# A three-layer feature-interaction network in fp32: half chunks moved to the front of a layer, products made two chunks wide

## The chip, the cores and the metric

The kernel runs on one core of a Trainium2 chip. The metric is the device time of one execution in microseconds (us); the time of a kernel is the median of its runs.

## The reference, cut to what matters

The input is 2048 samples of 39 fields with 16 channels, fp32. Each layer multiplies all pairs of a previous and an original field, channel by channel, and mixes the products with a learned matrix to 128 features. The first 64 features are kept, the other 64 feed the next layer.

```
z = relu(einsum('bhk,bmk,hmf->bfk', prev, x0, Wr) + b_i)   # i = 0, 1, 2
results.append(z[:, :64]); prev = z[:, 64:]                # prev = x0 for i = 0
y = sum_k(concatenate(results, axis=1)) @ W_lin
```

## The kernel before, in words

**Tiling.** The batch is cut into 32 blocks of 64 samples; a block is 1024 columns (16 channels x 64 samples). The contraction over pairs (h, m) is cut into chunks of up to 128 rows, one pair a row. For each chunk VectorE multiplies two 1024-column operands elementwise into a product, and TensorE multiplies the chunk's weights with it, 512 columns at a time. An fp32 matmul is two instructions in the profile.

**Layer 0** works on symmetric pairs of the input: 6 full chunks (x_rot, C0) and one half chunk (x_rot_s) that has 64 rows for each half of the columns. `split` does the two halves of such a chunk with two matmuls on rows 0 to 63 and 64 to 127 of the array, which can run side by side. `full` does two matmuls on all rows.

**Layers 1 and 2** have 20 chunks each (CH): 10 with the first spread of the previous layer's features (a = 0, t = 0 to 8, then T2), 9 with the second spread (a = 1), and last the chunk T1, which has 64 rows of work. In layer 1 it is a split chunk whose product VectorE makes with two instructions (L216); in layer 2 it is 64 rows high (L212). The other 19 are 128x1024 products (L210). Layer 2 keeps only 64 features, so its two column halves go to the two 64-column halves of the array and run side by side (L362). The products go through a ring of 10 slots (prod); VectorE waits for a free slot with chunk_used, TensorE for a product with prod_ready. layer2 waits at chunk 18 for the products of chunks 18 and 19 together (L359).

**Order, by engine.** It is written out by hand; each engine has its own program, and semaphores tie them. TensorE, per block i: layer 1 of i (76 full instructions at L323, 4 split at L317), layer 0 of block i+1 (split chunk first, then 24 full instructions), layer 2 of i (80 instructions). VectorE: products1(i), channel_sum2(i), products0(i+1) with the split product at L195 first, products2(i) with the channel sum of layers 0 and 1 (L258) after its chunk 11. ScalarE takes the results out of PSUM: evacuate1 writes the spread of layer 1 (prev; two ops at L404, four at L409) and the kept half (res01, L416), evacuate0 the same for layer 0, evacuate2 layer 2's (L434); weigh01 and weigh2 scale the sums into a pool. Layer 2's products can't start before evacuate1's first two ops. SP issues all input loads: load_pairs (operands of layer 0) when layer 0 has been done, load_bc (x_bc, fields repeated over partitions, double-buffered by block parity u) when VectorE has made layer 2's products.

**Start.** Block 0 has no x_bc loads: VectorE builds it from x_seed by shuffles (seed, L189), most of them between the products of layer 0. keep_warm issues matmuls on zeros.

**End.** The last layer 1 is put into the middle of layer 2 of the block before, after its chunk 10 (TAIL = 11 chunks before it, 9 behind it), so that TensorE has work while ScalarE spreads the result. At the very end two small matmul groups (L393), a copy and one store make the output.

Of the kernel before, what the change touches and what calls it, by code (L numbers as in the profile page):

```python
# [14 lines left out]
def cin_kernel(nc, x, w0, w0_mirror, w1, w2, b0, b1, b2, w_lin, out, dims):  # L15
# [14 lines left out]
    CH = len(CHUNKS)  # L30
    X0_GROUPS = [(0, 1), (1, 2), (2, 4), (4, C0)]
# [8 lines left out]
    BC_LOADS = [QPT] * len(XB_GROUPS) + [3]  # L40
    SMALL = 7
    TAIL = RING + 1
# [3 lines left out]
    with ExitStack() as ctx:  # L46
# [28 lines left out]
        res01 = sb("res01", [P, NB])  # L75
# [17 lines left out]
        w2_loaded = sem("w2_loaded")  # L93
        small_loaded = sem("small_loaded")
        ones_ready = sem("ones_ready")
        split_loaded = sem("split_loaded")
        rep_loaded = sem("rep_loaded")
# [4 lines left out]
        bc_loaded = [[sem(f"bc_loaded{u}{g}") for g in range(len(XB_GROUPS) + 1)]  # L102
# [3 lines left out]
        chunk_used = sem("chunk_used")  # L106
        acc0_full = sem("acc0_full")
# [14 lines left out]
        def _(sp):  # L122
# [5 lines left out]
            def load_pairs(i):  # L128

                for h in range(NH):  # L130
# [4 lines left out]
                    sp.dma_start(x_rot_s[rows, :], src).then_inc(split_loaded, 16)  # L135
                for r, n in ((0, 48), (48, 48), (96, ROWS0[0] - 96)):
                    sp.dma_start(x_rep[r:r + n, :], x[i, r % M:r % M + n, :]).then_inc(rep_loaded, 16)
# [8 lines left out]
            def load_bc(i, u):  # L146
# [5 lines left out]
                for q in range(2):  # L152
                    src = rows_of(i, QPT * T + q, [[0, HALF], [1, NB]])
                    sp.dma_start(x_bc[HALF * q:HALF * q + HALF, u, T2, :], src).then_inc(bc_loaded[u][-1], 16)
                src = rows_of(i, M - 1, [[0, P], [1, NB]])
                sp.dma_start(x_bc[:, u, T1, :], src).then_inc(bc_loaded[u][-1], 16)
# [5 lines left out]
            sp.wait_ge(acc0_full, 1)  # L162
            load_pairs(1)
            load_bc(1, 1)
            for i in range(U):
                sp.wait_ge(acc0_full, i + 2)
                load_pairs(i + 2)
                sp.wait_ge(prod_ready, i * (2 * CH) + 2 * CH)
                load_bc(i + 2, i)
            with sp.Fori(1, STEPS - 1) as j:  # L170
                for u in range(U):
                    i = j * U + u
                    sp.wait_ge(acc0_full, i + 2)
                    load_pairs(i + 2)
                    sp.wait_ge(prod_ready, i * (2 * CH) + 2 * CH)
                    load_bc(i + 2, u)
# [7 lines left out]
        def _(dve):  # L184
# [7 lines left out]
            def products0(i, seeds=()):  # L192

                dve.wait_ge(split_loaded, i * (32 * NH) + 32 * NH)
                nc.vector.tensor_tensor(x_rot_s[:], x_rot_s[:], x_rep_s[:], ALU.mult).then_inc(prod0_ready, 1)  # L195
                dve.wait_ge(rep_loaded, i * (16 * 3) + 16 * 3)
                for g, (c0, c1) in enumerate(X0_GROUPS):
                    dve.wait_ge(rot_loaded[g], i * (16 * ROT_LOADS[g]) + 16 * ROT_LOADS[g])
                    for c in range(c0, c1):
                        r = x_rot[0:ROWS0[c], c, :]  # L200
                        nc.vector.tensor_tensor(r, r, x_rep[0:ROWS0[c], :], ALU.mult).then_inc(prod0_ready, 1)  # L201
                        for t in seeds[c:c + 1]:
                            seed(t)

            def product(layer, c, u, slot):

                a, t = CHUNKS[c]
                old, new = prev[layer - 1][a], x_bc[:, u, t, :]
                if t < T1:
                    mul = nc.vector.tensor_tensor(prod[:, slot, :], old[:], new, ALU.mult)  # L210
                elif layer == 2:
                    mul = nc.vector.tensor_tensor(prod[0:HALF, slot, :], old[0:HALF, :], new[0:HALF], ALU.mult)  # L212
                else:
                    for h in range(NH):
                        k, n = slice(HALF * h, HALF * h + HALF), slice(BANK * h, BANK * h + BANK)
                        mul = nc.vector.tensor_tensor(prod[k, slot, n], old[k, n], new[k, n], ALU.mult)  # L216
                mul.then_inc(prod_ready, 1)

            def products1_seeded():

                spread_by = {T2: T + 2, T1: T + 3}
                for c, (a, t) in enumerate(CHUNKS):
                    if a == 0 or t == T1:
                        dve.wait_ge(seed_spread, spread_by.get(t, t + 1))
# [318 lines left out]
```

## Time and profile before

| | |
|---|---|
| Median of 3 runs | 2055.02 us (2054.32 to 2055.65) |
| Profiled execution, its own time | 2055.68 us |
| Its span | 2053.9 us |
| TensorE / weight loads | 2030.3 / 804.6 us busy (99% / 39%) |
| VectorE / ScalarE / GpSimd | 1809.6 / 539.0 / 1.2 us busy (88% / 26% / 0%) |
| Input loads | 307.71 MB, 68.7% of the DMA engines' time |
| Granted TensorE clock | 0.997 of full speed over the span |

The span is measured from the first to the last instruction in the trace; the device time holds 1.8 us more. In the profile PE is TensorE's matmuls, PEld its weight loads (they overlap the matmuls), DVE VectorE, ACT ScalarE, POOL GpSimd, SP the engine that issues loads. L323 is line 323. A matmul's listed duration (some 593 ns) holds its way through the array and is longer than the distance to the next one. "[0.76 <-issue]" behind a row is the idle time before it on its engine and what ended it.

### The profile page before, as it was taken

What the parts mean: (1) busy time and instruction counts of PE and PEld (TensorE: products, weight loads), DVE (VectorE), ACT (ScalarE), POOL (GpSimd) and SP (SyncE); (2) the same over time, 40 slices, a digit from 0 to 9 for tenths busy, and PEclk for the clock granted to TensorE, in tenths of its full rate; (3) what the DMA queues carried; (4) which work ended last, traced back from release to release, by engine and by line L of the source; (5) the groups of instructions that cost most, each with busy time, mean ns of one, the idle gap of its engine ahead of it and who ended that gap; (6) DMA issues with size and microseconds to landing.
All of it is one profiled execution on the core that took longest, in us unless ns stands there. A gap on an engine that the chain in (4) does not pass through costs nothing.

```text
span 2053.9 us, 20773 instructions
## 1 busy us (share of the span) xinstructions
PE 2030.3 (99%) x6050; PEld 804.6 (39%) x6050; DVE 1809.6 (88%) x1630; ACT 539.0 (26%) x547; POOL 1.2 (0%) x5
## 2 busy tenths in 40 slices
PE   7999999999999999999999999999999999999998
PEld 2344333443333443334433344333344333443342
DVE  6988988889988889888899888898888988889987
ACT  1331133311333212333113332123321233311322
POOL 0000000000000000000000000000000000000000
PEclk9999999999999999999999999999999999999999
DMA  8967866668766688666786666876668866668710
GB/s 199 199 146 163 179 145 140 148 146 190 158 130 150 144 176 169 150 139 144 157 190 142 140 147 143 187 166 133 147 145 168 183 141 141 145 148 190 152 38 0
DMA packets 98550, 308.99 MB, mean 150 GB/s; under 512 B 19252, under 2 KB 19252, under 8 KB 98408
## 3 DMA queue, kind: packets, MB, share of 16 engines
q1 hardware_dynamic: 97400, 307.71, 68.7%
q10 hardware_dynamic: 1136, 1.12, 0.2%
q8 instruction: 6, 0.10, 0.0%
q14 instruction: 8, 0.07, 0.0%
HBM read 308.74 MB, written 0.01 MB: 150 GB/s over the span
## 4 chain that ended last, share of the span: by engine, by line
PE 89%; DVE 6%; issue 3%; ACT 0%; DVEq 0%
PE acc L323 66%; PE acc L362 20%; DVE prod L210 4%; PE acc L317 3%; DVE prod L212 2%; ACT prev L404 0%; DVE sum L258 0%; DVE x_bc L189 0%; DVEq L241 0%; PE acc_y L393 0%; DVE x_rot L201 0%; ACT res L434 0%; DVE x_seed L305 0%; ACT pool L439 0%; DVEq L240 0%
## 5 line engine op out<-in xcount | busy, mean ns | idle before, releaser
L210 DVE TENSOR_TENSOR prod<-prev,x_bc 128x1024 f32<-128x1024 f32 x1216 | 1390.1, 1223 | 221.6 <-ACT prev L404 215.0
L323 PE MATMUL acc<-prod,w_sb 128*128 128x512 f32 x2432 | 1052.3, 593 | 0.3 <-DVE prod L210 0.3
L323 PEld LDWEIGHTS acc<-prod,w_sb 128*128 128x128 f32 x2432 | 459.4, 190 | 592.6 <-issue 546.8
L362 PE MATMUL acc<-prod,w_sb 128*64 128x512 f32 (+1 forms) x2560 | 569.3, 596 | 6.1 <-DVE prod L212 1.2
L323 PE MATMUL acc<-x_rot,w_sb 117*128 117x512 f32 (+1 forms) x768 | 341.0, 599 | 2.7 <-DVE x_rot L201 2.7
L362 PEld LDWEIGHTS acc<-prod,w_sb 128*64 128x64 f32 (+1 forms) x2560 | 175.3, 136 | 396.2 <-issue 320.1
L409 ACT ACTIVATE prev<-acc,bias 32x1024 f32<-32x1024 f32 x256 | 283.4, 1107 | 4.0
L404 ACT ACTIVATE prev<-acc,bias 64x1024 f32<-64x1024 f32 x128 | 142.0, 1109 | 498.6 <-PE acc L317 355.2
L201 DVE TENSOR_TENSOR x_rot<-x_rot,x_rep 117x1024 f32<-117x1024 f32 (+1 forms) x192 | 221.1, 1220 | 3.0 <-DMA x_rot<-x 2.9
L323 PEld LDWEIGHTS acc<-x_rot,w_sb 117*128 117x128 f32 (+1 forms) x768 | 143.4, 190 | 198.8 <-issue 189.7
L439 ACT ACTIVATE pool<-sum,wl_col 128x64 f32 (+1 forms) x65 | 22.1, 342 | 679.6 <-DVE sum L258 679.6
L258 DVE TENSOR_REDUCE sum<-res 128x64 f32<-128x512 f32 (+1 forms) x65 | 96.5, 1484 | 2.9 <-ACT res L434 2.0
L434 ACT ACTIVATE res<-acc,bias 128x512 f32<-128x512 f32 x32 | 22.1, 690 | 292.4 <-PE acc L362 292.4
L416 ACT ACTIVATE res<-acc,bias 64x1024 f32<-64x1024 f32 x64 | 70.9, 1108 | 26.6 <-DVE sum L258 25.0
L216 DVE TENSOR_TENSOR prod<-prev,x_bc 64x512 f32<-64x512 f32 x64 | 44.1, 689 | 0.9 <-PE acc L323 0.5
L317 PE MATMUL acc<-x_rot_s,w_sb 64*128 64x512 f32 x128 | 33.8, 606 | 8.7 <-DVE x_rot_s L195 8.7
L212 DVE TENSOR_TENSOR prod<-prev,x_bc 64x1024 f32<-64x1024 f32 x32 | 38.9, 1217 | 0.5 <-PE acc L323 0.5
L317 PE MATMUL acc<-prod,w_sb 64*128 64x512 f32 x128 | 36.1, 641 | 0.0
L317 PEld LDWEIGHTS acc<-x_rot_s,w_sb 64*128 64x128 f32 x128 | 12.5, 191 | 24.1 <-issue 24.1
L195 DVE TENSOR_TENSOR x_rot_s<-x_rot_s,x_rep_s 128x512 f32<-128x512 f32 x32 | 21.8, 682 | 0.0
L317 PEld LDWEIGHTS acc<-prod,w_sb 64*128 64x128 f32 x128 | 9.6, 184 | 24.3 <-issue 23.5
L189 DVE STREAM_SHUFFLE x_bc<-x_seed 128x1024 f32<-128x1024 f32 (+1 forms) x12 | 15.5, 1296 | 0.0
(17 smaller groups left out, 21.8 us busy)
## 6 DMA issues: line engine op xcount, KB each, us to landing
x_bc<-x SPq DMA_DIRECT2D x310, 256.0 KB, 13.1
x_bc<-x SPq DMA_DIRECT2D x155, 512.0 KB, 21.2
x_rot<-x SPq DMA_DIRECT2D x192, 312.0 KB
x_rot<-x SPq DMA_DIRECT2D x192, 156.0 KB
x_bc<-x SPq DMA_DIRECT2D x124, 128.0 KB, 8.9
x_rep<-x SPq DMA_DIRECT2D x64, 192.0 KB
x_rep_s<-x SPq DMA_DIRECT2D x64, 128.0 KB, 2.6
x_rot_s<-x SPq DMA_DIRECT2D x64, 128.0 KB, 2.8
```

The costliest lines, as they stand in the source:

```text
L201: nc.vector.tensor_tensor(r, r, x_rep[0:ROWS0[c], :], ALU.mult).then_inc(prod0_ready, 1)
L210: mul = nc.vector.tensor_tensor(prod[:, slot, :], old[:], new, ALU.mult)
L212: mul = nc.vector.tensor_tensor(prod[0:HALF, slot, :], old[0:HALF, :], new[0:HALF], ALU.mult)
L216: mul = nc.vector.tensor_tensor(prod[k, slot, n], old[k, n], new[k, n], ALU.mult)
L258: return nc.vector.tensor_reduce(total[:], res[:].rearrange("p (k b) -> p b k", b=BB), mybir.AxisListType.X, ALU.add)
L317: mm = nc.tensor.matmul(acc[:, h, :], w[k, :], rhs[h], start=start, stop=stop)
L323: mm = nc.tensor.matmul(acc[:, h, :], w, rhs[:, BANK * h:BANK * h + BANK], start=start, stop=stop)
L362: mm = nc.tensor.matmul(acc2[HALF * h:HALF * h + HALF, :], w2_sb[0:k, c, :], prod[0:k, c % RING, BANK * h:BANK * h + BANK], start=(c == 0) ...
L404: op = nc.scalar.activation(dst[0][HALF * g:HALF * g + HALF, :], src, ACT.Relu, bias=bias[HALF:P, layer:layer + 1])
L409: op = nc.scalar.activation(dst[1][QUAD * q:QUAD * q + QUAD, :], acc[h:h + QUAD, :, :].rearrange("p h n -> p (h n)"), ACT.Relu, bias=bias[ ...
L416: nc.scalar.activation(res01[HALF * layer:HALF * layer + HALF, :], acc[0:HALF, :, :].rearrange("p h n -> p (h n)"), ACT.Relu, bias=bias[0: ...
L434: nc.scalar.activation(res2[:], acc2[:], ACT.Relu, bias=bias[:, 2:3]).then_inc(res2_ready, 1)
```

## The change

- The chunks of layers 1 and 2 are taken in the order ORDER: chunk T1 first, then the others as before. RUNS groups them by position: 4 single chunks and 8 pairs. A pair is one VectorE product of 2 x 1024 columns whose first operand is repeated by a broadcast; prod_ready counts runs (12 a layer), chunk_used still counts chunks.
- TensorE does layer 1's split chunk first, and right behind it the split chunk of layer 0 of the next block (layer0_split); its other layer-0 chunks keep their place after layer 1. In block 0 and in the last layer 1 the two stay apart (ahead=False).
- VectorE makes the split product of layer 0 before products1. SP loads its operands on their own (load_split) when TensorE has used the old ones.
- The weights of layer 2's chunk T1 are set to zero in rows 64 to 127 (GpSimd, once), and its product and its matmul take all 128 rows.
- res01 has two buffers (the second is x_seed), and the channel sum of layers 0 and 1 of block i-1 is done in block i, between products0(i+1) and products2(i). weigh01 moves with it.
- TAIL is 12 chunks (8 runs) and the seeds of block 0 are dealt out anew.

The core of the diff (removed lines are mostly left out, they stand above):

```diff
     T2, T1 = T, T + 1
     CHUNKS = [(0, t) for t in range(T)] + [(0, T2)] + [(1, t) for t in range(T)] + [(0, T1)]
     CH = len(CHUNKS)
+    ORDER = [CH - 1] + list(range(CH - 1))
+    RUNS = [(0, 1), (1, 1), (2, 2), (4, 2), (6, 2), (8, 2), (10, 1), (11, 1), (12, 2), (14, 2), (16, 2), (18, 2)]
+    RUN_OF = [n for n, (_, w) in enumerate(RUNS) for _ in range(w)]
+    NR = len(RUNS)
...
-    BC_LOADS = [QPT] * len(XB_GROUPS) + [3]
+    BC_T1, BC_T2 = len(XB_GROUPS), len(XB_GROUPS) + 1
+    BC_LOADS = [QPT] * len(XB_GROUPS) + [1, 2]
     SMALL = 7
-    TAIL = RING + 1
+    TAIL_RUNS, TAIL = 8, 12
     LAST = NBLK - 1
...
         w0m_sb = prod[:, RING - 1, 0:(C0 + 1) * F].rearrange("p (c f) -> p c f", f=F)
-        res01 = sb("res01", [P, NB])
+        res01 = [sb("res01", [P, NB]), x_seed]
         res2 = sb("res2", [P, BANK])
...
+                sp.dma_start(x_bc[:, u, T1, :], src).then_inc(bc_loaded[u][BC_T1], 16)
+            load_split(0)
             load_pairs(0)
             sp.dma_start(w1_sb[:], w1).then_inc(w1_loaded, 16)
             sp.dma_start(w2_sb[:], w2).then_inc(w2_loaded, 16)
+            sp.wait_ge(split_used, 1)
             sp.wait_ge(acc0_full, 1)
...
+            sp.wait_ge(split_used, 2)
+            load_split(2)
+            sp.wait_ge(acc0_full, 2)
+            load_pairs(2)
+            sp.wait_ge(prod_ready, 2 * NR)
+            load_bc(2, 0)
+            sp.wait_ge(split_used, 3)
...
             with sp.Fori(1, STEPS - 1) as j:
                 for u in range(U):
                     i = j * U + u
+                    sp.wait_ge(split_used, i + 2)
+                    load_split(i + 2)
                     sp.wait_ge(acc0_full, i + 2)
+                    sp.sem_inc(pairs_asked, 1)
                     load_pairs(i + 2)
+                    sp.wait_ge(prod_ready, i * (2 * NR) + 2 * NR)
                     load_bc(i + 2, u)
             sp.wait_ge(y_copied, 1)
...
+            def product_split(i):
                 dve.wait_ge(split_loaded, i * (32 * NH) + 32 * NH)
                 nc.vector.tensor_tensor(x_rot_s[:], x_rot_s[:], x_rep_s[:], ALU.mult).then_inc(prod0_ready, 1)
...
+            def product(layer, n, u, phase=0):
+                pos, w = RUNS[n]
+                a, t = CHUNKS[ORDER[pos]]
+                s = (phase + pos) % RING
                 old, new = prev[layer - 1][a], x_bc[:, u, t, :]
+                if w == 2:
+                    twice = old[:].rearrange("p (o n) -> p o n", o=1).to_broadcast([P, w, NB])
+                    mul = nc.vector.tensor_tensor(prod[:, s:s + w, :], twice, x_bc[:, u, t:t + w, :], ALU.mult)
+                elif layer == 1 and t == T1:
+                    for h in range(NH):
+                        k, cols = slice(HALF * h, HALF * h + HALF), slice(BANK * h, BANK * h + BANK)
+                        mul = nc.vector.tensor_tensor(prod[k, s, cols], old[k, cols], new[k, cols], ALU.mult)
                 else:
+                    mul = nc.vector.tensor_tensor(prod[:, s, :], old[:], new, ALU.mult)
                 mul.then_inc(prod_ready, 1)
...
+                spread = {0: 1, 1: 2, 2: 4, 3: 6, 4: 8, 5: 10, 6: 12}
+                late = {2: (6,), 3: (7, 8), 4: (T2,)}
+                for n, (pos, w) in enumerate(RUNS):
+                    if n in spread:
+                        dve.wait_ge(seed_spread, spread[n])
+                    if pos in (0, 11):
+                        dve.wait_ge(prev_ready[0], 1 if pos == 0 else 2)
+                    dve.wait_ge(chunk_used, pos + w)
+                    product(1, n, 0)
...
+            def products2(i, u, first, part=range(NR)):
+                for n in part:
+                    pos, w = RUNS[n]
+                    if pos in (0, 11):
+                        dve.wait_ge(prev_ready[1], i * 2 + (1 if pos == 0 else 2))
+                    dve.wait_ge(chunk_used, first + pos + w)
+                    product(2, n, u)
...
+            def channel_sum01(i, a):
+                dve.wait_ge(res01_ready, i * 2 + 3)
+                channel_sum(sum01, res01[a]).then_inc(sum01_ready, 1)
...
             dve.wait_ge(w0_cleared, 1)
             nc.vector.tensor_tensor(w0_sb[:], w0_sb[:], w0m_sb, ALU.add).then_inc(w0_ready, 1)
+            product_split(0)
...
+            products0(0, [T1, 0, 1, 2, 3])
+            seed(4)
+            seed(5)
+            products1_seeded()
+            channel_sum2(0)
+            product_split(1)
+            products0(1)
+            products2(0, 0, CH)
+            product_split(2)
+            products1(1, 1, 1, 2 * CH)
+            channel_sum2(1)
+            products0(2)
+            channel_sum01(0, 0)
+            products2(1, 1, 3 * CH)
             with dve.Fori(1, STEPS - 1) as j:
                 for u in range(U):
                     i = j * U + u
+                    product_split(i + 1)
                     products1(i, u, j + u, i * (2 * CH))
                     channel_sum2(i)
                     products0(i + 1)
+                    channel_sum01(i - 1, 1 - u)
                     products2(i, u, i * (2 * CH) + CH)
             n = (LAST - 1) * (2 * CH)
+            product_split(LAST)
             products1(LAST - 1, 0, STEPS - 1, n)
             channel_sum2(LAST - 1)
             products0(LAST)
+            channel_sum01(LAST - 2, 1)
+            products2(LAST - 1, 0, n + CH, range(TAIL_RUNS))
             products1(LAST, 1, STEPS, n + CH + TAIL, TAIL)
+            products2(LAST - 1, 0, n + 2 * CH, range(TAIL_RUNS, NR))
+            channel_sum01(LAST - 1, 0)
             products2(LAST, 1, n + 3 * CH)
             channel_sum2(LAST)
+            channel_sum01(LAST, 1)
             channel_sum2(NBLK)
             dve.wait_ge(y_ready, 1)
...
             nc.gpsimd.memset(x_seed[:], 0.0).then_inc(seed_cleared, 1)
+            pool.wait_ge(seed_cleared, 1)
+            pool.wait_ge(w2_loaded, 16)
+            nc.gpsimd.memset(w2_sb[HALF:P, CH - 1, :], 0.0).then_inc(w2_ready, 1)
...
+            def layer0_split(i):
                 pe.wait_ge(prod0_ready, i * (C0 + 1) + 1)
+                split(acc0, w0_sb[:, C0, :], [x_rot_s[0:HALF, :], x_rot_s[HALF:P, :]],
+                      True, False).then_inc(split_used, 1)
+            def layer0(i):
                 for c in range(C0):
                     pe.wait_ge(prod0_ready, i * (C0 + 1) + c + 2)
                     k = ROWS0[c]
                     mm = full(acc0, w0_sb[0:k, c, :], x_rot[0:k, c, :], False, c == C0 - 1)
                 mm.then_inc(acc0_full, 1)
...
+            def layer1(i, runs, phase=0, ahead=True):
                 pe.wait_ge(res01_ready, i * 2 + 1)
+                for pos, c in enumerate(ORDER):
+                    pe.wait_ge(prod_ready, runs + RUN_OF[pos] + 1)
+                    s = (phase + pos) % RING
+                    if pos == 0:
+                        split(acc1, w1_sb[:, c, :], [prod[0:HALF, s, 0:BANK], prod[HALF:P, s, BANK:NB]],
+                              True, False).then_inc(chunk_used, 1)
+                        if ahead:
+                            pe.wait_ge(res01_ready, i * 2 + 2)
+                            layer0_split(i + 1)
                     else:
+                        full(acc1, w1_sb[:, c, :], prod[:, s, :], False, pos == CH - 1).then_inc(chunk_used, 1)
+            def layer2(i, runs, part=range(CH)):
                 pe.wait_ge(res2_ready, i + 1)
+                for pos in part:
+                    pe.wait_ge(prod_ready, runs + RUN_OF[pos] + 1)
                     for h in range(NH):
+                        mm = nc.tensor.matmul(acc2[HALF * h:HALF * h + HALF, :], w2_sb[:, ORDER[pos], :],
+                                              prod[:, pos % RING, BANK * h:BANK * h + BANK],
+                                              start=(pos == 0), stop=(pos == CH - 1))
...
+            layer0_split(0)
+            layer0(0)
             keep_warm(4)
...
+            layer1(0, 0, ahead=False)
+            pe.wait_ge(res01_ready, 2)
+            layer0_split(1)
+            layer0(1)
+            pe.wait_ge(w2_ready, 1)
+            layer2(0, NR)
+            layer1(1, 2 * NR)
+            layer0(2)
+            layer2(1, 3 * NR)
+            with pe.Fori(1, STEPS - 1) as j:
                 for u in range(U):
                     i = j * U + u
+                    layer1(i, i * (2 * NR))
                     layer0(i + 1)
...
+            n = (LAST - 1) * (2 * NR)
             layer1(LAST - 1, n)
             layer0(LAST)
+            layer2(LAST - 1, n + NR, range(TAIL))
+            layer1(LAST, n + NR + TAIL_RUNS, TAIL, ahead=False)
+            layer2(LAST - 1, n + 2 * NR, range(TAIL, CH))
+            layer2(LAST, n + 3 * NR)
...
+            def keep01(acc, layer, a):
...
+                act.wait_ge(sum01_ready, i + 3)
                 weigh(pool01, i * BB, sum01, 0)
...
+            weigh01(LAST - 2)
+            evacuate0(LAST, 1)
+            act.wait_ge(prod_ready, (LAST - 1) * (2 * NR) + 3 * NR)
+            evacuate1(LAST, 1, n + 2 * CH + TAIL)
             weigh01(LAST - 1)
             evacuate2(LAST - 1, n + 3 * CH)
             weigh2(LAST)
+            evacuate2(LAST, n + 4 * CH)
             weigh01(LAST)
```

## Rows read from the trace of the kernel before

**Rows 1.** Page, part 1: busy us (share of the span) xinstructions.

```profile
PE 2030.3 (99%) x6050; PEld 804.6 (39%) x6050; DVE 1809.6 (88%) x1630; ACT 539.0 (26%) x547; POOL 1.2 (0%) x5
```

**Rows 2.** Chain of waits, whole span: start us, length us, what.

```profile
38.31 32.88 PE acc L323 x76
101.34 32.81 PE acc L323 x76
...
1929.66 32.81 PE acc L323 x76
1984.48 32.83 PE acc L323 x76
```

**Rows 3.** Timeline, TensorE's weight loads: start us, length us, line, shape.

```profile
1016.67 0.30 PEld L317 LDWEIGHTS acc<-prod,w_sb 64*128 64x128 f32 x4 [0.76 <-issue]
...
1017.21 0.19 PEld L317 LDWEIGHTS acc<-x_rot_s,w_sb 64*128 64x128 f32 x2 [0.23 <-issue]
...
1017.64 0.19 PEld L317 LDWEIGHTS acc<-x_rot_s,w_sb 64*128 64x128 f32 x2 [0.23 <-issue]
...
1018.59 0.30 PEld L323 LDWEIGHTS acc<-x_rot,w_sb 124*128 124x128 f32 x2 [0.76 <-issue]
...
1019.13 0.19 PEld L323 LDWEIGHTS acc<-x_rot,w_sb 124*128 124x128 f32 x1 [0.24 <-issue]
...
1028.14 0.19 PEld L323 LDWEIGHTS acc<-x_rot,w_sb 117*128 117x128 f32 x1 [0.24 <-issue]
1029.09 0.20 PEld L362 LDWEIGHTS acc<-prod,w_sb 128*64 128x64 f32 x4 [0.76 <-issue]
...
1029.57 0.14 PEld L362 LDWEIGHTS acc<-prod,w_sb 128*64 128x64 f32 x2 [0.28 <-DVE prod L210]
```

**Rows 4.** Timeline, end of the same block's layer 2.

```profile
1043.62 1.22 DVE L212 TENSOR_TENSOR prod<-prev,x_bc 64x1024 f32<-64x1024 f32 x1
...
1044.89 0.20 PEld L362 LDWEIGHTS acc<-prod,w_sb 128*64 128x64 f32 x4 [1.01 <-DVE prod L212]
1045.90 0.19 PEld L362 LDWEIGHTS acc<-prod,w_sb 64*64 64x64 f32 x4 [0.81 <-issue]
1046.90 0.30 PEld L323 LDWEIGHTS acc<-prod,w_sb 128*128 128x128 f32 x2 [0.81 <-issue]
...
1047.44 0.19 PEld L323 LDWEIGHTS acc<-prod,w_sb 128*128 128x128 f32 x1 [0.24 <-issue]
```

**Rows 5.** Timeline, ScalarE and VectorE: layer 2's start, then layer 1's end.

```profile
1017.85 2.23 ACT L404 ACTIVATE prev<-acc,bias 64x1024 f32<-64x1024 f32 x2 [11.65 <-PE acc L317]
...
1020.20 12.58 DVE L210 TENSOR_TENSOR prod<-prev,x_bc 128x1024 f32<-128x1024 f32 x11 [7.06 <-ACT prev L404]
...
1066.32 1.39 DVE L216 TENSOR_TENSOR prod<-prev,x_bc 64x512 f32<-64x512 f32 x2
...
1068.68 0.68 DVE L195 TENSOR_TENSOR x_rot_s<-x_rot_s,x_rep_s 128x512 f32<-128x512 f32 x1
1069.28 6.90 DVE L201 TENSOR_TENSOR x_rot<-x_rot,x_rep 124x1024 f32<-124x1024 f32 x6
```

**Rows 6.** Timeline, VectorE in the first block.

```profile
37.03 5.77 DVE L210 TENSOR_TENSOR prod<-prev,x_bc 128x1024 f32<-128x1024 f32 x5 [3.22 <-issue]
...
42.72 1.30 DVE L189 STREAM_SHUFFLE x_bc<-x_seed 128x1024 f32<-128x1024 f32 x1
43.92 2.33 DVE L210 TENSOR_TENSOR prod<-prev,x_bc 128x1024 f32<-128x1024 f32 x2
```

**Rows 7.** Chain of waits after the last layer 1.

```profile
2018.59 1.11 ACT prev L404
...
2034.57 1.84 DVE sum L258
...
2045.54 2.11 PE acc L362 x8
```

More of the change, by code:

```diff
@@ L201, in products0 @@
                         nc.vector.tensor_tensor(r, r, x_rep[0:ROWS0[c], :], ALU.mult).then_inc(prod0_ready, 1)
[L202 to L207, printed above, removed]
-                old, new = prev[layer - 1][a], x_bc[:, u, t, :]
[L209 to L212, printed above, removed]
-                else:
-                    for h in range(NH):
-                        k, n = slice(HALF * h, HALF * h + HALF), slice(BANK * h, BANK * h + BANK)
-                        mul = nc.vector.tensor_tensor(prod[k, slot, n], old[k, n], new[k, n], ALU.mult)
+                        if c < len(seeds):
+                            seed(seeds[c])
@@ L232, in products1 @@
+                late = {2: (6,), 3: (7, 8), 4: (T2,)}
[6 more added lines that the diff above has]
+                    product(1, n, 0)
+                    for t in late.get(n, ()):
+                        seed(t)
             def products1(i, u, loads, first, phase=0):
@@ L234, in products1 @@
                 group = {t0: g for g, (t0, _) in enumerate(XB_GROUPS)}
[L235 to L236 removed]
+                group[T1], group[T2] = BC_T1, BC_T2
+                for n, (pos, w) in enumerate(RUNS):
+                    a, t = CHUNKS[ORDER[pos]]
                     if a == 0 and t in group:
                         dve.wait_ge(bc_loaded[u][group[t]], loads * (16 * BC_LOADS[group[t]]))
[L239 to L242 removed]
@@ L244, in products2 @@
-            def products2(i, u, first, part=range(CH)):
-                for c in part:
-                    a, t = CHUNKS[c]
-                    if t == 0:
-                        dve.wait_ge(prev_ready[1], i * 2 + a + 1)
-                    dve.wait_ge(chunk_used, first + c + 1)
-                    product(2, c, u, c % RING)
-                    if c == TAIL:
-                        dve.wait_ge(res01_ready, i * 2 + 3)
-                        channel_sum(sum01, res01).then_inc(sum01_ready, 1)
+                    if pos in (0, 11):
+                        dve.wait_ge(prev_ready[0], i * 2 + (1 if pos == 0 else 2))
@@ L354, in layer2 @@
-            def layer2(i, first, part=range(CH)):
-                pe.wait_ge(w2_loaded, 16)
+                for pos, c in enumerate(ORDER):
[7 more added lines that the diff above has]
+                            layer0_split(i + 1)
+                    else:
+                        full(acc1, w1_sb[:, c, :], prod[:, s, :], False, pos == CH - 1).then_inc(chunk_used, 1)
@@ L469, in _ @@
             act.wait_ge(small_loaded, 16 * SMALL)
-            evacuate0(0)
-            with act.Fori(0, STEPS - 1) as j:
+            evacuate0(0, 0)
+            for i in range(U):
+                weigh2(i)
+                evacuate1(i, i, i * (2 * CH) + CH)
+                evacuate0(i + 1, 1 - i)
+                if i > 0:
+                    weigh01(i - 1)
+                evacuate2(i, i * (2 * CH) + 2 * CH)
+            with act.Fori(1, STEPS - 1) as j:
                 for u in range(U):
```

113 lines of the change are left out of this document (28 added, 85 removed).

## The prediction

> **What bounds the kernel now.** I read the page's shares by engine first. TensorE is busy 99% of the span and VectorE 88% [rows 1], so time can only come from TensorE: from its own work, from small holes in it, or from the start and the end. The chain of waits then gives the rhythm. From the second block on, layer 1 begins every 63.04 us ((1929.66 - 101.34) / 29), the first block takes 63.03, the shortened next-to-last stretch 54.82, and what follows the last layer 1's start 69.4 [rows 2].
>
> Third, TensorE's weight loads at the seams of a block. One load stands beside each matmul instruction, so their starts give the pitch: (1028.14 - 1019.13) / 21 = 0.429 us [rows 3]. A block has 144 such slots: 76 (layer 1 full), 2 + 2 (the two half chunks, whose instructions run in pairs), 24 (layer 0 full), 40 (layer 2, in pairs). 144 x 0.4288 = 61.75 us. The other 1.29 us of 63.04 sits at the seams, and the reader can add it up in [rows 3, 4]. When the shape of the tiles in the array changes, the first slot is long (0.54, or 0.48 into layer 2, for 0.43) and the last before the change is followed by a gap. The seams are: into layer 1's half chunk 0.12 + 0.11 (layer 1 starts at 1046.90 - 63.04 = 983.86, so 76 slots and 0.11 end at 1016.55); from layer 0's half chunk to its full ones 0.09 + 0.11 (0.95 for two slots); into layer 2 0.10 + 0.05; into layer 2's last chunk 0.15 (1.01 for two slots); from it to layer 1 0.14 + 0.11. That is 0.98. The last 0.31 is a wait: chunk 18 of layer 2 should start at 1029.09 + 0.05 + 36 slots = 1044.58, and starts at 1044.89, behind the VectorE product of chunk 19, which ends at 1044.84 [rows 4] (layer2 waits for both products at chunk 18).
>
> VectorE is late there because its 20 products of layer 2 can start only when ScalarE has spread layer 1's result, at 1020.20, and follow each other every 1.136 us ((12.58 - 1.22) / 10), with a 1.84 us channel sum in the middle [rows 5, 7].
>
> **The change part by part.** I count from one point, Z: the first slot of layer 0's work after the end of layer 1 (1017.64 before [rows 3]). ScalarE starts 0.21 later and VectorE's first layer-2 product 2.56 later [rows 5]; I keep both.
>
> *Order of the chunks (TensorE).* New block: half chunk of layer 1, half chunk of next block's layer 0, 76 + 24 full slots, 40 slots of layer 2. Seams left: layer 2 to half chunks, half chunks to full, full to layer 2, priced 0.14 + 0.11, 0.09 + 0.11, 0.10 + 0.05 = 0.60. Layer 1's full slots run straight into layer 0's: before, both had 128-row tiles too, and the step from 124 to 117 rows inside layer 0 shows no gap. The seam between 64-column tiles and two 64-row tiles isn't in this trace. Its bounds are 0.05 (the cheapest entry alone) and 0.36 (all of 0.25 and another 0.11); I take 0.25, the row nearest to it, where row tiles are left or entered from a full array.
>
> *Layer 2's last chunk padded with zeros.* TensorE's slots keep their length, since 64-row and 128-row ones had the same pitch; VectorE's product has 1024 columns either way (1.22). It removes the mode change at 0.15 and, with its own wait, chunk 18's early wait for chunk 19. The memset is on idle POOL at the start.
>
> *Products two chunks wide (VectorE).* 8 of a layer's 12 instructions are pairs. A column costs 1/0.96 ns by the difference of a 1024-column (1.22) and a 512-column product (0.69) [rows 5], so a pair is 1.136 + 1.067 = 2.20. Lower bound 2.13 (columns alone), upper bound 2.45 (two separate full durations of 1.22). A layer takes 4 x 1.136 + 8 x 2.20 = 22.15.
>
> *Channel sum of layers 0/1.* Its 1.84 us leaves layer 2's products and goes where VectorE waits for ScalarE anyway: the hole before 1020.20 is 7.06 us [rows 5], so it's free; if that hole were gone it would cost its 1.84 on VectorE. The second result buffer keeps ScalarE from waiting for it.
>
> *Waits added.* With Z as zero: layer 0's full slots end at 10.39; layer 2's start there and end at 27.59 with the seam 27.73. VectorE ends its products at 2.56 + 22.15 + 0.09 = 24.8. TensorE wants the last pair at 10.44 + 15.44 = 25.9: 1.1 us to spare, where before it was 0.3 short. Then VectorE does the half-chunk product of layer 0 (0.68) and layer 1's two halves (1.39) [rows 5] and is ready at 26.8, wanted at 27.73: 0.95 to spare. Behind those two instructions stand all of layer 1's products; the second chunk is ready at 28.0, wanted at 29.6. A pair needs two free slots of the ring: pair (12,13) of layer 2 asks for chunk 3, consumed at 13.9, and is begun at 16.1, so the ring doesn't hold it. SP's queue: the half-chunk loads now wait behind the block's broadcast loads instead of standing ahead of the pair loads; both have most of a block until their product is made, and no steady product waited for a DMA. The new wait of layer 0's half chunk for ScalarE's last read of layer 0's result is met some 9 us early (eight ScalarE passes of 1.11 [rows 7] from 10.6).
>
> So a steady block is 61.75 + 0.60 = 62.35, 0.69 less (0.38 seams, 0.31 wait). 29 blocks: **-20.0**.
>
> *First block.* The seed shuffles (1.20 each, 42.72 to 43.92 [rows 6]) are dealt out anew; five, not four, stand inside layer 1, before runs that TensorE already wants. From 37.03: halves to 38.4, where TensorE starts (38.31 before); chunk 1 39.5; pair (2,3) 41.7; shuffle; (4,5) 45.1; two shuffles; (6,7) 49.7; two shuffles (T2); (8,9) 54.3. TensorE wants them at 39.4, 41.3, 45.2, 48.6 and 53.2: stalls 0.1 + 0.4 + 1.1 + 1.1, less what the seams give back. Layer 1 ends at 74.9 and not 72.2. With layer 2 shorter by 0.47 and a seam of 0.1 more before layer 0, block 1 starts **2.6** later. Bounds 0 (as before) and +5 (each shuffle exposed). That the first half chunk now runs at about 9 us and leaves TensorE idle until 18.5 I price at nothing: the products of layer 0 come every 2.3 us or more there.
>
> *Last stretches.* Next-to-last: 62.35 - 17.34 + 12 chunks of 0.858 + 0.15 = 55.45 for 54.82 (TAIL is 12 for 11): **+0.6**. After the last layer 1, VectorE's products set the end. Before: TensorE passes that layer's seam at 1984.48 + 32.8 + 1.0 = 2018.3, and starts the last two chunks at 2045.54 [rows 7], 27.25 later: 2.56 to the first product, 22.8 of products, 1.84 of sum, 0.05. Now the first product comes 2.46 after the seam (the seam's 0.10 is counted in), products take 22.15 + 0.09, and the sum stands behind them, beside TensorE's last 2.11 and ScalarE's 0.7: 24.75. **-2.5** (bounds -1.3, the sum still in the way for 1.2, and -3.2).
>
> Sum: -20.0 + 2.6 + 0.6 - 2.5 = -19.3. The profiled execution took 2055.68 (span 2053.9 and 1.8 around it), so 2036.4 for it; the median of the runs is 0.66 lower, 2055.02. I forecast 2035.7.
>
> The Trainium skill (TensorEngine Tiling (Array Packing), Key Properties) says that changing the tiling mode drains the engine, and TensorE: Matmul & The Clock Gate (Single matmul latency) puts the drain at about 175 ns. Before had five changes of mode, after has three; by the page's figure that is an estimate of 2 x 0.175 x 29 = 10.2 us for the seams, where the rows give 11.0, and the forecast would be 2036.5. The page leaves out the long first slot, which the rows show.
>
> **The rivals.**
>
> A, VectorE becomes the bound in layer 2 (the losing side). For it: only 0.95 us to spare, a pair is released as a whole, and no row shows a two-chunk product or an operand read twice. Against: columns and pitch leave little to add. It decides from 2.20 + 0.95/8 = 2.32 a pair; from 2.41 the stall eats the 0.69. At 2.45 the stall is 8 x 0.25 - 0.95 = 1.05, a block 0.36 longer than before: 29 x 0.36 = +10.4, first block +3.6, last stretches 0: about 2069.
>
> B, the seams stay: the full-to-full step between layers or the unseen seam costs what the two removed ones did. For it: no row has that seam. Then only the 0.31 wait goes: -9.0 + 2.6 + 0.6 - 2.5 = -8.3, 2046.7.
>
> C, the first block costs more, its bound of +5: 2038. For it: four stalls in a row that I chained.
>
> D, a load arrives late because of its new place in SP's queue, or the waits do something I don't see. 0.5 us a block would give 2050.
>
> **How the numbers follow.** Forecast 0.74, C 0.08, B 0.10, A 0.05, D 0.03. The forecast's own spread: first block -2.6/+1.5, tail +-1, the unseen seam -5.8/+3.2. Range 2030 to 2043: it leaves out A, D and most of B. About 0.2% (4 us) is what a measurement of this kernel tells from no change. Faster 0.94 (all but A and half of D), same 0.02, slower 0.04.
>
> **What would show it.** Layer-1 starts 62.35 apart; weight loads at 0.43 straight across the end of layer 1; no TensorE wait for VectorE in layer 2; pairs at 2.20 (VectorE group of 2048 columns at about 2.29 each); TensorE idle some 2 to 3 us in the first block; the last two chunks starting about 24.8 after the last layer 1. The forecast is wrong if a pair is over 2.32, if a gap of 0.2 stands between the layers' full chunks, or if the block is not near 62.35.

## The result and the profile after

The changed kernel takes 2037.97 us (median of 4 runs, 2036.55 to 2040.70), beside 2054.73 us for the kernel before on the same chips: ratio 0.9919, 95% interval 0.9902 to 0.9937. Run again in the experiments it took 2036.74 (0.9911, 0.9894 to 0.9927). The forecast was 2035.7 in 2030 to 2043.

The ratio's interval leaves out 1, so the gain of 0.8% is real. The profiled execution took 2036.55 (span 2034.8), where the forecast for a profiled one was 2036.4. Shares by engine, the answer to [rows 1]:

```profile
PE 2012.9 (99%) x6050; PEld 812.5 (40%) x6050; DVE 1773.4 (87%) x1118; ACT 539.0 (26%) x547; POOL 1.3 (0%) x6
```

TensorE is 17.4 us less busy, though it runs as many instructions (x6050): a matmul's listed duration (some 593 ns, 429 ns from start to start) reaches over a short hole, so the holes at the seams had counted as busy. VectorE has 512 instructions less.

The chain of waits in a steady block and at its last ones, for [rows 2]:

```profile
1039.54 1.92 PE acc L363 x8
1041.45 43.12 PE acc L369 x100
1084.57 17.32 PE acc L408 x80
...
1912.48 1.92 PE acc L363 x8
...
1967.97 1.06 PE acc L363 x4
1969.03 32.83 PE acc L369 x76
```

In the steady blocks the chain now stays on TensorE. From 1039.54: the two half chunks 1.92, then layers 1 and 0 in one piece of 100 instructions, 43.12, then layer 2. In the 29 blocks to 1912.48 the period is (1912.48 - 104.24) / 29 = 62.35 us, 63.04 before; 104.24 is where block 1 starts in the same view.

The weight loads at a block's start, for [rows 3, 4]:

```profile
1039.47 0.30 PEld L363 LDWEIGHTS acc<-prod,w_sb 64*128 64x128 f32 x4 [0.81 <-issue]
1040.00 0.19 PEld L363 LDWEIGHTS acc<-x_rot_s,w_sb 64*128 64x128 f32 x2 [0.24 <-issue]
1040.43 0.19 PEld L363 LDWEIGHTS acc<-x_rot_s,w_sb 64*128 64x128 f32 x2 [0.23 <-issue]
1041.38 0.30 PEld L369 LDWEIGHTS acc<-prod,w_sb 128*128 128x128 f32 x2 [0.76 <-issue]
1041.92 0.19 PEld L369 LDWEIGHTS acc<-prod,w_sb 128*128 128x128 f32 x1 [0.24 <-issue]
```

Half chunks: 0.96 and 0.95 for two slots each, then a long first slot of 0.54 into the full chunks. The seam that no row of before had, 64-column tiles to two 64-row tiles, shows as the weight loader's idle 0.81 before 1039.47, the same as at the old seam out of layer 2, and a first slot of 0.53. And the step from layer 1 (prod) to layer 0 (x_rot):

```profile
1073.25 0.19 PEld L369 LDWEIGHTS acc<-prod,w_sb 128*128 128x128 f32 x1 [0.24 <-issue]
1073.68 0.19 PEld L369 LDWEIGHTS acc<-x_rot,w_sb 124*128 124x128 f32 x1 [0.24 <-issue]
```

0.43, with no seam. VectorE at the end of layer 2, for [rows 4, 5]:

```profile
1034.27 2.29 DVE L239 TENSOR_TENSOR prod<-prev,x_bc 128x2048 f32<-128x2048 f32 x1
1036.47 0.69 DVE L218 TENSOR_TENSOR x_rot_s<-x_rot_s,x_rep_s 128x512 f32<-128x512 f32 x1
1037.07 1.38 DVE L243 TENSOR_TENSOR prod<-prev,x_bc 64x512 f32<-64x512 f32 x2
1038.48 1.22 DVE L245 TENSOR_TENSOR prod<-prev,x_bc 128x1024 f32<-128x1024 f32 x1
```

The instruction behind a pair starts 2.20 after it (1034.27 to 1036.47), though the pair is listed with 2.29. The halves for layer 1 are ready at 1038.45 (1037.07 + 1.38), and TensorE takes them at 1039.47: 1.0 to spare.

TensorE in the first block (the same view of layer 1 in the kernel before lists one hole, of 0.27), and the chain of waits behind the last layer 1, for [rows 6, 7]:

```profile
38.18 1.13 PE L363 MATMUL acc<-prod,w_sb 64*128 64x512 f32 x4 [0.52 <-DVE prod L243]
...
41.55 7.13 PE L369 MATMUL acc<-prod,w_sb 128*128 128x512 f32 x16 [0.22 <-DVE prod L239]
49.58 3.70 PE L369 MATMUL acc<-prod,w_sb 128*128 128x512 f32 x8 [0.90 <-DVE prod L239]
54.50 5.85 PE L369 MATMUL acc<-prod,w_sb 128*128 128x512 f32 x13 [1.22 <-DVE prod L239]
```

```profile
2001.94 1.11 ACT prev L460
...
2004.21 2.36 DVE prod L245 x2
...
2017.65 8.81 DVE prod L239 x4
2026.45 2.79 DVE sum L286 x2
...
2029.76 2.04 PE acc_y L449 x16
```

The holes in brackets, 0.22 + 0.90 + 1.22, stand where the forecast put its stalls. At the end both channel sums (2.79) stand behind the products. What the forecast did not have is TensorE's own wait of 1.93 before the last layer 2, for ScalarE's result of the block before. The second view holds the weight load of the last two chunks:

```profile
2001.77 7.09 PE L408 MATMUL acc<-prod,w_sb 128*64 128x512 f32 x32
2010.79 17.65 PE L408 MATMUL acc<-prod,w_sb 128*64 128x512 f32 x80 [1.93 <-ACT res L490]
```

```profile
2026.51 0.20 PEld L408 LDWEIGHTS acc<-prod,w_sb 128*64 128x64 f32 x4 [0.93 <-DVE prod L239]
```

The last two chunks start 24.74 us after the seam behind the last layer 1 (2001.77), for 24.75 forecast, and what they wait for is VectorE's last pair. So in this execution the 1.93 is not on the path: TensorE has caught up by then and waits once more.

### The profile page after: what moved, and what is told of

Its sections match the earlier page's. It is cut to its first block, busy times and chain, and to the rows that moved or that the text cites. A ratio compares the mean times of both kernels' runs of the same rounds, so it can differ in the third digit from the quotient of the medians.

```text
span 2034.8 us, 19288 instructions
## 1 busy us (share of the span) xinstructions
PE 2012.9 (99%) x6050; PEld 812.5 (40%) x6050; DVE 1773.4 (87%) x1118; ACT 539.0 (26%) x547; POOL 1.3 (0%) x6
## 4 chain that ended last, share of the span: by engine, by line
PE 96%; DVE 2%; issue 0%; ACT 0%; DVEq 0%; ACTq 0%
PE acc L369 67%; PE acc L408 26%; PE acc L363 3%; DVE prod L239 1%; DVE x_bc L212 1%; DVE prod L245 0%; DVE sum L286 0%; ACT prev L460 0%; PE acc_y L449 0%; DVE x_rot L227 0%; DVE x_seed L348 0%; ACT pool L495 0%; DVE prod L243 0%; DVEq L257 0%; ACTq L483 0%
## 5 line engine op out<-in xcount | busy, mean ns | idle before, releaser
L239 DVE TENSOR_TENSOR prod<-prev,x_bc 128x2048 f32<-128x2048 f32 x512 | 1139.0, 2287 | 7.1 <-PE acc L369 7.1
L408 PE MATMUL acc<-prod,w_sb 128*64 128x512 f32 x2560 | 556.8, 593 | 2.0 <-ACT res L490 1.9
L245 DVE TENSOR_TENSOR prod<-prev,x_bc 128x1024 f32<-128x1024 f32 x224 | 265.5, 1221 | 231.5 <-ACT prev L460 230.5
L408 PEld LDWEIGHTS acc<-prod,w_sb 128*64 128x64 f32 x2560 | 180.8, 137 | 374.0 <-issue 333.8
L286 DVE TENSOR_REDUCE sum<-res 128x64 f32<-128x512 f32 (+1 forms) x49 | 64.4, 1314 | 0.0
L472 ACT ACTIVATE res<-acc,bias 64x1024 f32<-64x1024 f32 x32 | 35.5, 1109 | 0.8
L472 ACT ACTIVATE x_seed<-acc,bias 64x1024 f32<-64x1024 f32 x32 | 35.5, 1109 | 0.8
L286 DVE TENSOR_REDUCE sum<-x_seed 128x64 f32<-128x1024 f32 x16 | 30.4, 1901 | 0.0
```

The costliest lines, as they stand in the source:

```text
L239: mul = nc.vector.tensor_tensor(prod[:, s:s + w, :], twice, x_bc[:, u, t:t + w, :], ALU.mult)
L245: mul = nc.vector.tensor_tensor(prod[:, s, :], old[:], new, ALU.mult)
L286: return nc.vector.tensor_reduce(total[:], res[:].rearrange("p (k b) -> p b k", b=BB), mybir.AxisListType.X, ALU.add)
L408: mm = nc.tensor.matmul(acc2[HALF * h:HALF * h + HALF, :], w2_sb[:, ORDER[pos], :], prod[:, pos % RING, BANK * h:BANK * h + BANK], start=( ...
L472: nc.scalar.activation(res01[a][HALF * layer:HALF * layer + HALF, :], acc[0:HALF, :, :].rearrange("p h n -> p (h n)"), ACT.Relu, bias=bias ...
```

## The experiments

**1. Padding alone.** The kernel before, with

```diff
-                    k = P if c < CH - 1 else HALF
+                    k = P
...
-                    mul = nc.vector.tensor_tensor(prod[0:HALF, slot, :], old[0:HALF, :], new[0:HALF], ALU.mult)
+                    mul = nc.vector.tensor_tensor(prod[:, slot, :], old[:], new, ALU.mult)
```

and the weights of that chunk zeroed in rows 64 to 127.

> The kernel before with one part of the change: layer 2's last chunk padded with zero weights to 128 rows, its joint wait at chunk 18 kept. Theory (seams and one wait): only the change of tile shape at 0.15 us leaves layer 2, so 31 x 0.15 = 4.7 us less than before, and the wait of about 0.3 us for VectorE's product of chunk 19 stays, or grows by what the seam gave back if VectorE is the bound there (then 0 us gained in steady blocks). Rival (the gain is VectorE's relief): no difference, since VectorE does the same work.

Measured: 2052.03, beside 2055.86 for the kernel before, ratio 0.9981 (0.9971 to 0.9990); 3.8 us less. Layer 1 starts every 62.93 us, 0.12 less. The rival is out. That it is 0.12 and not 0.15 shows in the weight loads at chunk 18:

```profile
1042.89 0.20 PEld L366 LDWEIGHTS acc<-prod,w_sb 128*64 128x64 f32 x4 [1.04 <-DVE prod L213]
1043.38 0.14 PEld L366 LDWEIGHTS acc<-prod,w_sb 128*64 128x64 f32 x2 [0.29 <-issue]
```

A wait has its own long first slot: 1042.89 to 1043.38 is 0.49 for 0.43. In [rows 4] I had booked that 0.05 to the change of tiles. It belongs to the wait. The rest of the change of tiles is 0.10 to 0.12.

**2. Padding, and each chunk waits for its own product.** One more edit:

```diff
-                    if c < CH - 1:
-                        pe.wait_ge(prod_ready, first + (c + 1 if c < CH - 2 else CH))
+                    pe.wait_ge(prod_ready, first + c + 1)
```

> The kernel before with the padded last chunk, and chunks 18 and 19 of layer 2 each waiting for their own product only. Theory: the seam (0.15) and the wait (0.31) leave every block, 30 x 0.47 = 14.1 us, and TensorE's last chunk but one starts earlier at the end (about 0.9): 15 us less than before, 2039.7, layer-1 starts 62.58 us apart, without any new order, pairs or moved sum. Rival (VectorE is the bound at layer 2's end and the moved sum and the pairs are what helps): 5 us or less gained.

Measured: 2039.63, ratio 0.9918 (0.9902 to 0.9935), 16.2 less than before on the same chip, where 15 was expected; between the two profiled executions it is 15.2 (2055.68 and 2040.46). Chain of waits, layer 1 of blocks 1 and 30:

```profile
101.18 32.81 PE acc L327 x76
...
1915.09 32.81 PE acc L327 x76
```

(1915.09 - 101.18) / 29 = 62.55. The wait was worth 62.93 - 62.55 = 0.38 a block (0.31, the long slot 0.05, rounding), more than any seam. These two small edits of the old order bring nearly all of the time that the whole change brings (2039.63 against 2036.7 to 2038.0). Their steady block is 0.20 longer, but they pay nothing in the first one: block 1 starts at 101.18 here and at 104.24 in the changed kernel. VectorE was not the limit as such: its 20th product was in time for chunk 19, and too late only for chunk 18, which did not need it.

**3. Layer 0's half chunk back behind layer 1.**

```diff
-            def layer1(i, runs, phase=0, ahead=True):
+            def layer1(i, runs, phase=0, ahead=False):
...
                     layer1(i, i * (2 * NR))
+                    pe.wait_ge(res01_ready, i * 2 + 2)
+                    layer0_split(i + 1)
                     layer0(i + 1)
```

Layer 0 of blocks 2 and 31 outside the loop is edited in the same way.

> The changed kernel with layer 0's half chunk taken back behind layer 1 in every block (layer 1's half chunk still leads). Theory: a full-to-half and a half-to-full change of tiles come back between the layers, 0.12 + 0.11 + 0.09 + 0.11 = 0.43 us a block less nothing: 29 blocks, +12.5 us on the changed kernel, starts 62.78 apart. Rival (full chunks of two layers in a row save nothing by themselves): within 2 us of the changed kernel.

Measured: 2049.66, ratio to before 0.9969 (0.9958 to 0.9980), 11.7 to 12.9 us above the changed kernel's two medians; starts 62.75 apart, 0.40 more (0.43 expected). The seams are back:

```profile
1078.29 0.19 PEld L369 LDWEIGHTS acc<-prod,w_sb 128*128 128x128 f32 x1 [0.24 <-issue]
1079.24 0.30 PEld L363 LDWEIGHTS acc<-x_rot_s,w_sb 64*128 64x128 f32 x4 [0.76 <-issue]
1080.30 0.30 PEld L369 LDWEIGHTS acc<-x_rot,w_sb 124*128 124x128 f32 x2 [0.76 <-issue]
1080.84 0.19 PEld L369 LDWEIGHTS acc<-x_rot,w_sb 124*128 124x128 f32 x1 [0.24 <-issue]
```

From the last load of layer 1 (1078.29) to the half chunk 0.95 where two slots are 0.86; two slots of the half chunk 1.06; a first slot of 0.54. Two changes of tiles cost 0.198 each. The Trainium skill (TensorEngine Tiling (Array Packing), Key Properties) says that a change of tiling mode drains the engine, and TensorE: Matmul & The Clock Gate (Single matmul latency) gives some 175 ns for the drain of a single matmul. That is 0.02 from the 0.198 here; that the two are the same thing isn't shown.

**4. The channel sum back inside layer 2's products.**

```diff
                     product(2, n, u)
+                    if n == 7 and late is not None:
+                        channel_sum01(i - 1, late)
```

The call ahead of layer 2's products is gone in these blocks.

> The changed kernel with the channel sum of layers 0/1 put back inside layer 2's products (behind the 8th of 12 runs) in blocks 2 to 29. Theory (VectorE has 1.0 us to spare at the end of layer 2): 1.84 us more there gives a stall of about 0.9 us a block, 28 blocks, +25 us on the changed kernel, with TensorE's waits for VectorE products in the profile. Rival (VectorE's place isn't critical after the change): no difference.

Measured: 2063.16, ratio to before 1.0034 (1.0023 to 1.0046): slower than the kernel before. Starts 63.23 apart, 0.88 more (0.9 expected). VectorE and TensorE in one layer 2 of it:

```profile
1039.54 1.94 DVE L288 TENSOR_REDUCE sum<-res 128x64 f32<-128x1024 f32 x1
1041.39 8.90 DVE L239 TENSOR_TENSOR prod<-prev,x_bc 128x2048 f32<-128x2048 f32 x4
```

```profile
1048.14 1.94 PE L409 MATMUL acc<-prod,w_sb 128*64 128x512 f32 x8 [0.16 <-DVE prod L239]
1050.34 1.94 PE L409 MATMUL acc<-prod,w_sb 128*64 128x512 f32 x8 [0.27 <-DVE prod L239]
```

The sum stands before the last four pairs, and TensorE waits for the last two. The bracket says 0.16 and 0.27, but the group before 1050.34 started 2.20 earlier for four slots of 0.43, so 0.48 was lost: the listed end of a matmul hides about 0.2 of each wait. The waits view sums these to 11.9 us in this kernel, a half of the 24.6 us (28 x 0.88) that the period lost; in the kernel before it showed none of the 0.3.

**5. Products one chunk wide.**

```diff
-    RUNS = [(0, 1), (1, 1), (2, 2), (4, 2), (6, 2), (8, 2), (10, 1), (11, 1), (12, 2), (14, 2), (16, 2), (18, 2)]
+    RUNS = [(n, 1) for n in range(CH)]
```

The end (TAIL_RUNS = 12) and the places of the shuffles are renumbered to stay at the same chunks.

> The changed kernel with every product one chunk wide (20 runs a layer in place of 12; shuffles of block 0 at the same chunks). Theory: steady blocks stay at 62.35 us, since VectorE's 1.0 us to spare covers 8 x 0.07 more; the first block stalls about 1.2 us less because a chunk is released by itself; the end is about 0.3 shorter: 1.5 us less than the changed kernel. Rival (the pairs carry a good part of the gain): 5 us or more slower than the changed kernel.

Measured: 2036.51, ratio 0.9914 (0.9897 to 0.9930), beside 2036.74 for the changed kernel on the same chip: 0.2 less, where 1.5 was expected, and the rival is out. Steady blocks 62.35: the pairs bring nothing there. Block 1 starts 1.4 us earlier than in experiment 7 (102.66 for 104.10), but 0.6 of it is luck: layer 1 of block 0 could start that much earlier (37.47 for 38.10), ahead of anything that the edit touches. The block itself is 0.8 shorter, for 1.2 expected. The end of the profiled execution, from the seam behind the last layer 1, was 1.4 us longer (34.4 for 33.0). That is TensorE's clock. Stretches around the start of the last layer 2 (columns: stretch, its us, busy of PE, PEld, DVE, ACT, POOL with instructions, granted clock, DMA share, GB/s), and weight loads:

```profile
2000.00:2009.00 9.00, 7.28 (x33) 2.21 (x32) 6.38 (x6) 8.51 (x9) 0.00 (x0) 1.00 0.01 2
2009.00:2014.00 5.00, 4.78 (x16) 1.49 (x18) 5.00 (x6) 0.16 (x1) 0.00 (x0) 0.66 0.00 0
2014.00:2019.00 5.00, 5.00 (x26) 1.69 (x24) 5.00 (x6) 0.00 (x0) 0.00 (x0) 1.00 0.00 0
```

```profile
2009.21 0.20 PEld L408 LDWEIGHTS acc<-prod,w_sb 128*64 128x64 f32 x4 [2.82 <-ACT res L490]
...
2010.77 0.24 PEld L408 LDWEIGHTS acc<-prod,w_sb 128*64 128x64 f32 x2 [0.61 <-issue]
2011.63 0.24 PEld L408 LDWEIGHTS acc<-prod,w_sb 128*64 128x64 f32 x2 [0.61 <-issue]
...
2014.40 0.14 PEld L408 LDWEIGHTS acc<-prod,w_sb 128*64 128x64 f32 x2 [0.28 <-issue]
2014.83 0.14 PEld L408 LDWEIGHTS acc<-prod,w_sb 128*64 128x64 f32 x2 [0.28 <-issue]
```

Mean granted clock 0.66 in the stretch behind the wait for ScalarE: the loads stand 0.86 apart, at 1.2 GHz, up to 2013, and 0.43 later, at 2.4 GHz. The last layer 2 took 19.1 us for 17.6 in the changed kernel's profile, whose clock stayed at 1.0 there. Experiments 3 and 4 have the same fall in their profiles (0.66 over the 5 us behind the wait), and the same longer end: 34.4 and 34.5 us from that seam to the span's end (2048.0 - 2013.62, 2061.4 - 2026.94). Since their code at the end is the changed kernel's, the fall costs 1.4 us. It came in three of the six profiles with this wait.

**6. The shuffles of block 0.**

```diff
             seed(5)
+            seed(6)
...
-                late = {2: (6,), 3: (7, 8), 4: (T2,)}
+                late = {3: (7,), 4: (8,), 5: (T2,)}
```

The seventh shuffle stays where it was; the eighth and T2's move one run back.

> The changed kernel with the shuffles of block 0 dealt out so that the sixth goes into VectorE's idle 2.0 us before the first layer 1 and the others stand one run later. Theory: TensorE's stalls in the first layer 1 (0.2 + 0.9 + 1.2 us) go, 2.1 us less than the changed kernel. Rival (the first block isn't on the path, or its start is set by something else): no difference.

Measured: 2034.69, ratio 0.9902 (0.9886 to 0.9919); 2.05 below the changed kernel on the same chip. TensorE in layer 1 of block 0:

```profile
37.99 1.13 PE L364 MATMUL acc<-prod,w_sb 64*128 64x512 f32 x4 [0.52 <-DVE prod L243]
...
41.36 19.15 PE L370 MATMUL acc<-prod,w_sb 128*128 128x512 f32 x44 [0.22 <-DVE prod L239]
```

From 41.36 it runs to the end without a hole; the 0.22 before it, which the theory also wanted gone, stays. Four runs of each overlap (2033.70 to 2036.09 and 2035.58 to 2037.88), but the traces settle it: from the start of layer 1 in block 0 to that of block 1 it takes 63.41 us (37.99 to 101.40), and 66.00 in experiment 7 (38.10 to 104.10). That is 2.6 less; the median shows 2.05 of it.

**7. The changed kernel again.**

> The changed kernel unchanged, for where its runs differ by 4 us. If the loads at the start vary, the start of layer 1 in block 1 moves with the span and the period stays 62.35; if a steady margin is sometimes missed, the periods differ from block to block and TensorE waits for VectorE in some of them.

Measured: 2036.74 (2035.58 to 2037.88). Period 62.35 in all blocks, as in the first profile, and layer 1 of block 1 within 0.2 us of it. In this profile, too, the clock stayed at 1.0 at the end. So no steady margin is missed; its 8 runs lie between 2035.58 and 2040.70, and neither profile is of one of the longest. The loads at the start do move the time a little: the profiles of experiments 3, 4, 9 and 10, whose code in the first block is the changed kernel's, have block 1 at 104.20, 104.66, 103.82 and 103.36.

**8 to 10. The end.** The ScalarE edit (8 with the shuffles of 6, 9 alone) and the filler (10):

```diff
-            evacuate1(LAST, 1, n + 2 * CH + TAIL)
+            act.wait_ge(chunk_used, n + 2 * CH + TAIL + RING)
+            spread(prev[1], acc1, 1)
             weigh01(LAST - 1)
             evacuate2(LAST - 1, n + 3 * CH)
+            keep01(acc1, 1, 1)
```

```diff
+            for _ in range(2):
+                nc.tensor.matmul(acc_y[:], w1_sb[:, 0, :], w1_sb[:, 0:4, :].rearrange("p c f -> p (c f)"),
+                                 start=True, stop=True)
             layer2(LAST, n + 3 * NR)
```

> The kernel of the seed experiment with one more edit: in the last stretch ScalarE takes layer 2's result of the block before ahead of the kept half of layer 1, not behind it. Theory (TensorE's 1.9 us without work before the last layer 2 sometimes costs it its full clock, as the 0.66 in the stretch behind it shows in three of the runs so far): the wait shrinks to about 0.8, the weight loads stay 0.43 apart, the median falls by 0.5 to 1 us and the runs come closer together; against the changed kernel 3 us less, 2034. Rival (VectorE's products set the end anyway): the median as in the seed experiment, the same spread.

> The changed kernel with that edit alone. Theory: 0.5 to 1.5 us less than the changed kernel in the median, up to 1.7 in a run that would have lost the clock. Rival: no difference.

> The changed kernel with two matmuls on weights (four instructions, 1.7 us, result unused) put into TensorE's idle 1.9 us before the last layer 2; the wait itself stays. Theory (it's the idle time that lets the clock fall): granted clock 1.0 through the last layer 2 in the profile, time as with the ScalarE edit. Rival (the clock falls there for another reason, or it costs nothing): as the changed kernel, with a spread of 4 us.

Measured: 8: 2034.32 (2033.17 to 2035.21), ratio 0.9896 (0.9879 to 0.9912), the lowest median of all, but only 0.4 below experiment 6, which ran on another chip. 9: 2036.61 (2036.13 to 2037.65), ratio 0.9909. 10: 2036.28 (2035.70 to 2037.30), ratio 0.9907. The changed kernel has 0.9919 and 0.9911: no difference between these is clear of the intervals, and the 0.5 to 1.5 us expected of 9 did not show. TensorE before and in the last layer 2, in 3 (the clock falls), in 9 and in 10:

```profile
2022.64 19.08 PE L408 MATMUL acc<-prod,w_sb 128*64 128x512 f32 x80 [1.94 <-ACT res L496]
```

```profile
2001.35 7.09 PE L408 MATMUL acc<-prod,w_sb 128*64 128x512 f32 x32
2009.38 14.24 PE L408 MATMUL acc<-prod,w_sb 128*64 128x512 f32 x64 [0.94 <-ACT res L490]
2023.88 1.94 PE L408 MATMUL acc<-prod,w_sb 128*64 128x512 f32 x8 [0.26 <-DVE prod L239]
2026.08 1.94 PE L408 MATMUL acc<-prod,w_sb 128*64 128x512 f32 x8 [0.26 <-DVE prod L239]
```

```profile
2007.91 1.98 PE L444 MATMUL acc_y<-w_sb 128*128 128x512 f32 x4
2009.92 17.65 PE L408 MATMUL acc<-prod,w_sb 128*64 128x512 f32 x80
```

The wait shrinks from 1.93 to 0.94 in 9, and is filled in 10; the granted clock is 1.00 in both behind it. But with the clock up neither edit gains anything. In 9 TensorE starts the last layer 2 sooner and then waits for VectorE's last two pairs. From the seam behind the last layer 1 to the span's end it takes 33.0 us in 9 and in 10 (2034.3 - 2001.35, 2033.9 - 2000.90), the same as in the changed kernel (2034.8 - 2001.77). So the rival of experiment 8 holds there: VectorE's products set the end. The edits can only save the 1.4 us of an execution that would lose the clock. That they do is not proven by three profiles without a fall (8, 9, 10), when three of the six with the full wait had none either.

Why some runs of the changed kernel are longer stays open. Its eight runs span 5.1 us. The start moved by 1.3 us from profile to profile (103.36 to 104.66), and a fall of the clock costs 1.4; that makes 2.7, and no run near 2040 us was profiled.

## Why the prediction was right, point by point

- *Steady block.* 0.69 less a block forecast, 62.35; measured 62.35. Its parts by the runs: the early wait 0.38 (forecast 0.31), the padded chunk 0.12 (0.15), the order of the chunks 62.55 - 62.35 = 0.20 (0.23). The long slot behind a wait (0.05), booked in the wrong place, is most of the difference. All parts were read off one measured 1.29, so what is booked under the wrong part leaves the sum as it is. Times 29 that is -20.0.
- *Seams.* Full chunks of two layers in a row cost nothing, and the unseen seam was as dear as the old one (0.25 taken, bounds 0.05 and 0.36). Rival B (2046.7) is out by the trace, and by experiment 3, which brings two changes of tiles back and takes 11.7 to 12.9 us longer.
- *Pairs.* 2.20 forecast and measured, 1.0 us to spare for 0.95. Rival A is out, yet it was near: experiment 4 takes 1.84 of that time back and ends slower than the kernel before, with 0.88 a block where the margin says 1.84 - 0.95 = 0.89. The pairs themselves were given too much weight: without them the steady block is the same.
- *Moved sum.* It was costed as free where it went, and is. In the new order it is what the gain rests on (experiment 4); in the old order it could stay (experiment 2).
- *First block.* +2.6 forecast. Block 1 starts at 104.24 for 101.34 [rows 2]: +2.9, although layer 1 of block 0 started 0.1 earlier. So the block was 0.4 under-priced. The stalls came where they were put, and experiment 6 took 2.6 back in the trace. Rival C (+5 here, 2038) is out by this, though its 2038 happens to be the first median: the number alone would have spoken for the wrong one of the two.
- *Next-to-last stretch.* 55.45 forecast, 55.49 measured (1912.48 to 1967.97): +0.7 for +0.6.
- *End.* -2.5 forecast; from the seam behind the last layer 1 to the span's end 35.6 before (2053.9 - 2018.3), 33.0 now (2034.8 - 2001.8): -2.6. VectorE's products set it, as forecast. TensorE's wait of 1.93 was not foreseen (the kernel before lists one of 0.87 at the same place, with no effect either); that it costs nothing with the clock up is luck for the forecast.
- *Loads and waits.* Rival D is out: every steady block of the two profiles has 62.35 or 62.36.
- *The sum.* -19.3 forecast for the profiled execution, -19.1 measured. The medians: -19.3 forecast, -16.8 and -18.5 measured. The forecast took the median to be 0.66 below the profiled execution, as before; the first median stands 1.42 above it. Why is open. TensorE's wait before the last layer 2, behind which some executions lose the full clock and 1.4 us, can be a part of it, but the four runs lie up to 4.2 us apart and no profile is of one of the longest.

## What to carry to other kernels

When the bounding engine shows 99%, count its slots: pitch (the distance from one matmul's start to the next) times their number, against the period, and then walk the starts of its weight loads over each seam. Here 1.29 us of 63 came to light so, and a single wait that asked for one product too many was the largest of them; look at what each wait of the bounding engine really needs before the order of the work is rebuilt. A wait that a profile lists costs time only if the chain runs over it: the 1.93 us before the last layer 2 could be cut or filled without a gain while the clock stayed up. When an edit lengthens an engine's work near the bound, work out its time to spare at the last hand-over in us; here 1.84 us more work against 0.95 to spare gave 0.89 forecast and 0.88 measured.

## What the runs showed of the hardware

- A change between array tile shapes costs TensorE about 0.2 us beside matmuls of 0.43: a gap of 0.09 to 0.14 and a first slot that is 0.11 too long (0.05 into 64-column tiles). By experiment 3 it is 0.198 each.
- A wait costs it 0.05 us more than its length (0.49 for 0.43 behind it), and the idle time that the profile lists for it is about 0.2 us too short, so short waits aren't listed at all.
- Two equal VectorE products of 1024 columns joined into one of 2048 save 0.07 us (2.20 for 2 x 1.136), though each alone lists 1.22.
- Behind TensorE's idle 1.9 us before the last layer 2 the granted clock was 0.66 over 5 us (first 1.2 GHz with weight loads 0.86 apart, then 2.4 GHz with 0.43) in three of the six profiles that have that idle time (experiments 3, 4 and 5; not in 6, 7 and the first), and 1.00 where the idle time was 0.9 (8 and 9), 1.0 (1 and 2) or filled (10). The fall costs 1.4 us here.
